# Writing out the expert loop and reordering the first two steps of a Strassen-type mixture-of-experts kernel

## The chip, the cores and the metric

The kernel runs on one core of a Trainium2 chip. The time is the device time of one execution in microseconds (us), lower is better. The comparison is the median of several executions.

## The reference, cut to what matters

The first half of the program is a layer norm and a Fourier-domain cross attention over 32 sequences of 512 rows; the change doesn't touch it. The second half is a mixture of experts. Every token is normalised, sent to the one of 8 experts with the highest logit, if that expert still has room (capacity 1024), run through that expert, scaled by its probability and added to its residual:

```python
h = jax.nn.gelu(jnp.einsum('ech,ehi->eci', dispatch, wi), approximate=False)   # (8,1024,512) x (8,512,2048)
expert_out = jnp.einsum('eci,eih->ech', h, wo)                                  # (8,1024,2048) x (8,2048,512)
combined = weight[:, None] * expert_out[top1, slot]
out = (residual + combined).reshape(inputs.shape)
```

## The kernel before

**Two stages.** The attention stage writes the rows of all tokens, sorted by expert, to `slots` in memory. The function `experts` then opens a block of its own in which each engine has its own instruction stream. All timestamps below from 1973 us on belong to that block.

**Tiling.** An expert's 1024 tokens are two groups of 512 (`n`, `g`), its inner 2048 are eight steps per group (`j`) of two halves of 128. So an expert is 16 steps (`i`), and the stage has 128 steps, numbered `q`. A step's first matrix product (tokens by `wi`) is done as a Strassen-type product of 2 by 2 blocks with seven block products. Each block product is 6 matmuls of 128x128 weights against 256 columns: both operands are split into a high and a low part, and the three products high-high, low-high and high-low run over two slices of the contraction (`product`, L1412). The second product (`down`, L1471 to L1473) is 24 matmuls of 512 columns per step, into the banks `out_ps[0..3]`, which gather over the 8 steps of a group.

**Engines.** TensorE (PE) does the products and turns (transposes) the normalised tokens of the next group (`turn`, L1404), four blocks `c` of four transposes. ScalarE (ACT) rounds operands to their high parts (`weights_high`, `weight_sums_high`, `down_weights_high`, `tokens_high`), normalises (`norm`, L1519), applies gamma and beta to a turned block (`affine`, L1529), copies partial sums between banks (`seed_x`, `seed_w`, `keep_fifth`) and does the gelus. VectorE (DVE) forms the block sums (`weights_add`, L1753 to L1759; `tokens_add`, L1720 to L1725), the low parts (`weights_low` and others) and two additions that close a step (`add_22`, L1788, and `add_12`, L1795). SyncE issues the loads, GpSimd the scattered stores.

**The order within a step** is written out by hand in each engine's `step`. On TensorE step `q` is: `first_products(q)` (12 matmuls, y and v banks), `last_product(q-1)` (6, w bank), `down(q-2)` part 0, a turn in steps 1 to 4 of a group, sixth and second product, `down(q-2)` part 1, the late products, `down(q-2)` parts 2 and 3. `first_products(q)` waits for `add_12(q-1)` and the weights of `q`; `last_product(q)` waits for `add_22(q)`; the turn waits for `fifth_ready(q)`, set by `keep_fifth(q)` behind `seed_x(q)` on ScalarE.

**Loops.** On TensorE, ScalarE, VectorE and SyncE the first and the last expert are written out, and the six between are a loop of the engine (`Fori(1, 7)`) whose body is the 16 steps of one expert. GpSimd has a loop over 7 experts.

**The beginning of the stage.** TensorE marks two banks, then turns the first group's four blocks one after the other through the single bank `v_bank`: block `c+1` waits until ScalarE's `affine` has read block `c`. ScalarE then makes the four high parts of the tokens, VectorE their sums and low parts, and only then do both begin step 0, in which they prepare the weights of step 1.

## Time and profile before

| What | Value |
|---|---|
| Median of 3 executions | 3416.19 us (3410.73 to 3417.0) |
| The profiled execution | 3416.19 us |
| Its span, first to last instruction | 3414.4 us |
| Busy share of TensorE | 96% |
| Mean granted clock of TensorE | 0.984 |

The span is about 1.8 us shorter than the time of the same execution. In the rows below PE is TensorE's matmuls, PEld its weight loads, DVE VectorE, ACT ScalarE, POOL GpSimd. "idle before" is the time in which the engine did nothing before an instruction, with what ended it; "issue" there means that nothing the profile shows was waited for, and PEq is the sequencer of PE. A granted clock of 1.00 is 2.4 GHz and 0.50 is 1.2 GHz.

### The profile page before, as it was taken

The numbers are of one execution on the slowest core, as the hardware profiler recorded it, in microseconds if no ns is written. First come the engines' busy times: TensorE is split into PE (matmuls) and PEld (weight loads), VectorE is DVE, ScalarE is ACT, GpSimd is POOL, SyncE is SP. The second block draws the span as 40 slices with busy tenths as digits, with TensorE's granted clock in tenths as the row PEclk, the third lists the DMA queues.
The fourth block names the chain that finished last, engine by engine and source line by source line (L and its number), as shares of the span: only waits on it lengthen the run. The fifth ranks groups of instructions, "written<-read, shape, count | busy, mean of one in ns | idle before, by whom it ended". The sixth has DMA issues, their size and how long they took to land. (4 is left out here: it accounts for less than half of the span.)

```text
span 3414.4 us, 56375 instructions
## 1 busy us (share of the span) xinstructions
PE 3264.1 (96%) x17944; PEld 2687.3 (79%) x17944; DVE 2868.4 (84%) x3953; ACT 2241.4 (66%) x4838; POOL 1416.3 (41%) x1608
## 2 busy tenths in 40 slices
PE   7999999999999999999999669999999999999998
PEld 5777777777777777777777359998989898989997
DVE  4999999999999999999999757776767776767774
ACT  5666666676666666676666367776767676767764
POOL 3476767677676767676775500000000000000001
PEclk9999999999999999999999779999999999999999
DMA  6422221222121222212120233344434433333331
GB/s 227 148 100 75 88 74 62 74 75 86 62 86 62 87 74 75 92 59 83 62 100 26 75 107 111 109 123 124 125 113 124 125 124 101 112 113 111 123 98 42
DMA packets 299962, 327.61 MB, mean 96 GB/s; under 512 B 47600, under 2 KB 179056, under 8 KB 299760
## 3 DMA queue, kind: packets, MB, share of 16 engines
q1 hardware_dynamic: 284400, 308.12, 28.5%
q0 software_dynamic: 15360, 16.99, 1.4%
q8 instruction: 104, 1.70, 0.2%
q14 instruction: 98, 0.80, 0.1%
HBM read 256.96 MB, written 101.97 MB: 105 GB/s over the span
## 5 line engine op out<-in xcount | busy, mean ns | idle before, releaser
L1369 POOL TENSOR_TENSOR tally<-tally,unit 1x1 f32<-1x1 f32 x16 | 8.4, 523 | 1314.6 <-DVE res L1814 1314.6
L1471 PE MATMUL out_ps<-wo_h,act_h 128*128 128x512 f32 x1024 | 405.1, 396 | 0.0
L1472 PE MATMUL out_ps<-wo_h,act_l 128*128 128x512 f32 x1024 | 404.5, 395 | 0.0
L1473 PE MATMUL out_ps<-wo_l,act_h 128*128 128x512 f32 x1024 | 399.6, 390 | 0.0
L1803 DVE TENSOR_TENSOR act_l<-act,act_h 128x512 fp32r<-128x512 f32 x256 | 176.5, 690 | 257.3 <-ACT act_h L1638 257.2
L1773 DVE TENSOR_TENSOR wi_l<-w_sum,wi_h 128x1024 fp32r<-128x1024 f32 x128 | 156.9, 1226 | 116.5 <-ACT wi_h L1570 115.4
L1412 PE MATMUL y_bank<-tok_h,wi_h 128*128 128x256 f32 x768 | 222.2, 289 | 13.9 <-DVE tok_l L1739 6.3
L972 POOL DMA_INDIRECT slots<-rows,slot_i x128 | 212.3, 1659 | 46.5 <-issue 46.2
L1473 PEld LDWEIGHTS out_ps<-wo_l,act_h 128*128 128x128 f32 x1024 | 193.4, 189 | 43.4
L511 PE MATMUL pair<-w_qh,q_high 128*128 128x512 f32 x512 | 222.2, 434 | 1.5 <-ACT q_low L743 1.5
L1471 PEld LDWEIGHTS out_ps<-wo_h,act_h 128*128 128x128 f32 x1024 | 195.1, 191 | 29.4
L1412 PE MATMUL y_bank<-tok_h,wi_l 128*128 128x256 f32 x768 | 217.5, 283 | 0.0
L1412 PE MATMUL y_bank<-tok_l,wi_h 128*128 128x256 f32 x768 | 217.2, 283 | 0.0
L1472 PEld LDWEIGHTS out_ps<-wo_h,act_l 128*128 128x128 f32 x1024 | 195.0, 190 | 25.9
L737 ACT ACTIVATE c_high<-xt_ps 128x512 fp32r<-128x512 f32 x128 | 76.3, 597 | 207.8 <-PE pair L511 146.3
L511 PE MATMUL pair<-w_vh,c_high 128*128 128x512 f32 x512 | 202.8, 396 | 5.3 <-DVE s L1083 4.1
L511 PE MATMUL pair<-w_kh,c_high 128*128 128x512 f32 x512 | 205.9, 402 | 0.0
L863 POOL TENSOR_TENSOR neg<-sum,minus_inv_dim 128x4 f32<-128x4 f32 x64 | 52.8, 825 | 363.6 <-ACT unused L666 358.0
L511 PE MATMUL pair<-w_ql,q_high 128*128 128x512 f32 x512 | 200.6, 392 | 0.0
L511 PE MATMUL pair<-w_kl,c_high 128*128 128x512 f32 x512 | 200.1, 391 | 0.0
L511 PE MATMUL pair<-w_qh,q_low 128*128 128x512 f32 x512 | 199.8, 390 | 0.0
L511 PE MATMUL pair<-w_vh,c_low 128*128 128x512 f32 x512 | 199.6, 390 | 0.0
(241 smaller groups left out, 11237.1 us busy)
## 6 DMA issues: line engine op xcount, KB each, us to landing
w_raw<-in_L_ffn_wi SPq DMA_DIRECT2D x256, 256.0 KB, 3.0
w_raw<-in_L_ffn_wo SPq DMA_DIRECT2D x128, 512.0 KB, 4.8
w_raw<-in_x SPq DMA_DIRECT2D x32, 1024.0 KB, 5.2
w_raw<-in_ctx SPq DMA_DIRECT2D x32, 1024.0 KB, 5.2
x_res<-in_x SPq DMA_DIRECT2D x31, 1024.0 KB, 5.3
out<-x_res SPq DMA_DIRECT2D x31, 1024.0 KB, 4.4
slots<-rows SPq DMA_DIRECT2D x4, 4160.0 KB, 16.6
got<-slots SPq DMA_DIRECT2D x15, 1040.0 KB, 7.6
```

Source lines behind the costliest of these rows:

```text
L511: last = nc.tensor.matmul(pair[k % 2][:, s, :], spec[:, c, tile * 256 + s * P:tile * 256 + (s + 1) * P], w[:, c, :], start=(c == 0 and n = ...
L737: nc.scalar.activation((c_high, q_high)[w][:, u, :], xt_ps[u % 2][:], ACT.Copy).then_inc(f1_high, 1)
L863: c.step(tv(neg[:], total[:], k["minus_inv_dim"], ALU.mult))
L972: nc.gpsimd.indirect_dma_start(slots, bass.IndirectOffsetOnAxis(ap=slot_i[p][:, t:t + 1].bitcast(u32), axis=0), rows[p][:, t, :], None, bo ...
L1369: nc.gpsimd.tensor_tensor(tally[:], tally[:], unit[:], ALU.add).then_inc(tallied, 1)
L1412: last = nc.tensor.matmul(dst, x[w][:, a, k, :], y[g][:, b, k, :], start=start and k == 0 and x is wi_h and y is tok_h, stop=False, skip_g ...
L1471: nc.tensor.matmul(out_ps[t][:], ah, oh, start=(j == 0 and h == 0), stop=False)
L1472: nc.tensor.matmul(out_ps[t][:], al, oh, start=False, stop=False)
L1473: last = nc.tensor.matmul(out_ps[t][:], ah, ol, start=False, stop=(j == STEPS - 1 and h == 1))
L1773: v.tensor_tensor(wi_l[i % 2][:, 3:7], w_sum[:], wi_h[i % 2][:, 3:7].bitcast(f32), ALU.subtract).then_inc(wi_low, 1)
L1803: v.tensor_tensor(act_l[i % INNER_RING][:, two], act32[:, two], act_h[i % INNER_RING][:, two].bitcast(f32), ALU.subtract).then_inc(done, 1)
```

## The change

It has four parts.

1. TensorE, ScalarE and VectorE get all 8 experts written out (`for e in range(EXPERTS)` of the program text in place of the engine's loop). SyncE and GpSimd keep their loops.
2. The first group's four turned blocks go to four banks, `out_ps[0..3]`, which nothing else uses yet, so a block no longer waits for the one before to be read. ScalarE applies gamma and beta to blocks 0 and 1, VectorE to blocks 2 and 3 (`affine_first`). `tokens_high` part 0 of group 0 now waits for all four blocks, and `tokens_add(0)` stands ahead of `tokens_low(0, 0, 0)`.
3. The work for step 1's weights moves from step 0 to before it: `weights_add(1)` ahead of `affine_first` on VectorE, `weights_high(1)` between the tokens' high parts on ScalarE, `weights_low(1)` behind the tokens' low parts.
4. For steps 0 and 1 (`CLOSED = 2`) TensorE runs `last_product(q)` at the end of step `q`'s late products, and not after the first products of step `q+1`.

```diff
--- before.py
+++ after.py
@@ -1308,6 +1308,7 @@
         res_ready, mixed_ready, mixed_stored = sem("res_ready"), sem("mixed_ready"), sem("mixed_stored")
 
         LAST = EXPERTS * 2 * STEPS
+        CLOSED = 2
 
         def on(q):
 
@@ -1395,13 +1396,14 @@
                     first = isinstance(n, int) and n == 0
                     if not first:
                         pe.wait_ge(normed_ready, n * GT + GT)
-                    wait(pe, tok_ready, n * CB + c)
                     if not first:
+                        wait(pe, tok_ready, n * CB + c)
                         pe.wait_ge(fifth_ready, q + 1)
+                    bank = out_ps[c] if first else v_bank
                     for t in range(GT):
                         if first and c == 0:
                             pe.wait_ge(normed_ready, t + 1)
-                        last = nc.tensor.transpose(v_bank[:, t * P:(t + 1) * P], normed[:, t, c * P:(c + 1) * P], eye[:])
+                        last = nc.tensor.transpose(bank[:, t * P:(t + 1) * P], normed[:, t, c * P:(c + 1) * P], eye[:])
                     last.then_inc(tr_mm, 1)
 
                 def product(dst, q, i, a, b, start=False):
@@ -1479,7 +1481,8 @@
                     before, early = (i - 1) % 16, (i - 2) % 16
                     n_early = e * 2 + (i - 2) // STEPS
                     first_products(q, n, i)
-                    last_product(q - 1, before)
+                    if q - 1 >= CLOSED:
+                        last_product(q - 1, before)
                     down(q - 2, n_early, early, 0)
                     if on(q) and 1 <= j <= CB:
                         turn(n + 1, j - 1, q)
@@ -1487,19 +1490,17 @@
                     second_product(q, i)
                     down(q - 2, n_early, early, 1)
                     late_products(q, i)
+                    if q < CLOSED:
+                        last_product(q, i)
                     down(q - 2, n_early, early, 2)
                     down(q - 2, n_early, early, 3)
 
                 mark_banks()
                 for c in range(CB):
                     turn(0, c, 0)
-                for i in range(16):
-                    step(0, i)
-                with pe.Fori(1, EXPERTS - 1) as e:
+                for e in range(EXPERTS):
                     for i in range(16):
                         step(e, i)
-                for i in range(16):
-                    step(EXPERTS - 1, i)
                 step(EXPERTS, 0)
                 step(EXPERTS, 1)
 
@@ -1526,14 +1527,15 @@
                     act.wait_ge(tr_mm, n * CB + c + 1)
                     if c == 0:
                         wait(act, tok_low, n * 4 - 1)
-                    nc.scalar.activation(tok32[:, c, :], v_bank[:], ACT.Identity, bias=bet[:, c:c + 1],
+                    bank = out_ps[c] if isinstance(n, int) and n == 0 else v_bank
+                    nc.scalar.activation(tok32[:, c, :], bank[:], ACT.Identity, bias=bet[:, c:c + 1],
                                          scale=gam[:, c:c + 1]).then_inc(tok_ready, 1)
 
                 def tokens_high(n, g, part):
                     if not group_on(n):
                         return
                     if part == 0:
-                        act.wait_ge(tok_ready, n * CB + 2)
+                        act.wait_ge(tok_ready, n * CB + (4 if isinstance(n, int) and n == 0 else 2))
                         wait(act, p4_mm, (n - 1) * STEPS)
                         nc.scalar.activation(tok_h[g][:, B21:B22 + 1], halves(tok32[:, 0:2, :]), ACT.Copy).then_inc(tok_high, 1)
                     elif part == 1:
@@ -1656,7 +1658,8 @@
                     inner_high(q - 1, before, 0)
                     gelu_21(q - 1)
                     inner_high(q - 1, before, 1)
-                    weights_high(q + 1, after)
+                    if q > 0:
+                        weights_high(q + 1, after)
                     seed_w(q, i)
                     gelu_11(q)
                     weight_sums_high(q + 1, after)
@@ -1686,19 +1689,14 @@
                 norm(0, 0)
                 affine(0, 0)
                 affine(0, 1)
-                affine(0, 2)
-                affine(0, 3)
                 tokens_high(0, 0, 0)
                 tokens_high(0, 0, 1)
+                weights_high(1, 1)
                 tokens_high(0, 0, 2)
                 tokens_high(0, 0, 3)
-                for i in range(16):
-                    step(0, i)
-                with act.Fori(1, EXPERTS - 1) as e:
+                for e in range(EXPERTS):
                     for i in range(16):
                         step(e, i)
-                for i in range(16):
-                    step(EXPERTS - 1, i)
                 step(EXPERTS, 0)
 
             @block.vector
@@ -1708,6 +1706,11 @@
                 def halves(rows):
 
                     return bass.AP(rows.tensor, rows.offset, [list(rows.ap[0]), [TOK, 2], [GROUP, 2], [1, TOK]])
+
+                def affine_first(c):
+                    dve.wait_ge(tr_mm, c + 1)
+                    v.tensor_scalar(tok32[:, c, :], out_ps[c][:], gam[:, c:c + 1], bet[:, c:c + 1],
+                                    ALU.mult, ALU.add).then_inc(tok_ready, 1)
 
                 def tokens_add(n):
 
@@ -1818,8 +1821,9 @@
                     q = e * 16 + i
                     j, g, n = i % STEPS, i // STEPS, e * 2 + i // STEPS
                     before, after = (i - 1) % 16, (i + 1) % 16
-                    weights_add(q + 1, after, 0)
-                    weights_add(q + 1, after, 1)
+                    if q > 0:
+                        weights_add(q + 1, after, 0)
+                        weights_add(q + 1, after, 1)
                     inner_low(q - 1, before, 0)
                     if j == 2:
                         mix(n - 1, 1 - g, (2, 3))
@@ -1836,7 +1840,8 @@
                     inner_low(q - 1, before, 1)
                     if j == 1:
                         mix(n - 1, 1 - g, (0,))
-                    weights_low(q + 1, after)
+                    if q > 0:
+                        weights_low(q + 1, after)
                     weight_sums_low(q + 1, after)
                     add_22(q, i)
                     add_12(q, i)
@@ -1849,18 +1854,19 @@
                 weights_low(0, 0)
                 weight_sums_low(0, 0)
                 down_weights_low(0, 0)
+                weights_add(1, 1, 0)
+                weights_add(1, 1, 1)
+                affine_first(2)
+                affine_first(3)
+                tokens_add(0)
                 tokens_low(0, 0, 0)
-                tokens_add(0)
                 tokens_low(0, 0, 1)
                 tokens_low(0, 0, 2)
                 tokens_low(0, 0, 3)
-                for i in range(16):
-                    step(0, i)
-                with dve.Fori(1, EXPERTS - 1) as e:
+                weights_low(1, 1)
+                for e in range(EXPERTS):
                     for i in range(16):
                         step(e, i)
-                for i in range(16):
-                    step(EXPERTS - 1, i)
                 for i in range(3):
                     step(EXPERTS, i)
```

## Rows read from the trace of the kernel before

**Rows 1.** The page, busy time and instructions, and the granted clock in 40 slices.

```profile
PE 3264.1 (96%) x17944; PEld 2687.3 (79%) x17944; DVE 2868.4 (84%) x3953; ACT 2241.4 (66%) x4838; POOL 1416.3 (41%) x1608
...
PEclk9999999999999999999999779999999999999999
```

**Rows 2.** Waits, engine PE, 2020 to 3414 us: total, times, longest.

```profile
PE v_bank L1412 <- issue: 12.1, 5, 2.9
PE y_bank L1412 <- issue: 3.1, 5, 0.9
```

**Rows 3.** Stretches; columns: length, busy (instructions) by engine, PEclk, DMA share, GB/s.

```profile
2013.00:2016.00 3.00, 3.00 (x12) 2.71 (x12) 1.40 (x4) 2.15 (x5) 0.00 (x0) 0.50 0.84 230
2150.00:2325.00 175.00, 175.00 (x1105) 158.05 (x1104) 127.79 (x207) 125.60 (x228) 12.98 (x10) 1.00 0.38 115
2337.00:2343.00 6.00, 3.34 (x20) 3.15 (x19) 1.98 (x5) 1.46 (x4) 0.00 (x0) 0.78 0.56 147
3220.00:3376.00 156.00, 156.00 (x988) 141.22 (x986) 109.07 (x174) 108.11 (x198) 12.69 (x10) 1.00 0.32 94
```

**Rows 4.** Timeline, PE: start us, us, instruction, [idle before it <- releaser].

```profile
2046.67 0.28 PE L1412 MATMUL v_bank<-tok_h,wi_h 128*128 128x256 f32 x1
...
2164.35 0.28 PE L1412 MATMUL v_bank<-tok_h,wi_h 128*128 128x256 f32 x1
...
2218.78 0.28 PE L1412 MATMUL v_bank<-tok_h,wi_h 128*128 128x256 f32 x1
...
2336.80 0.38 PE L1412 MATMUL y_bank<-tok_h,wi_h 128*128 128x256 f32 x1 [0.90 <-issue]
...
2340.91 0.37 PE L1412 MATMUL v_bank<-tok_h,wi_l 128*128 128x256 f32 x1 [2.66 <-issue]
...
3219.75 0.28 PE L1412 MATMUL v_bank<-tok_h,wi_h 128*128 128x256 f32 x1
```

**Rows 5.** DMA queues, 2165 to 2335 us, the two of instruction code: packets, MB, share.

```profile
q8 instruction: 9, 0.15, 0.4%
q14 instruction: 9, 0.07, 0.1%
```

**Rows 6.** Waits, engine DVE, 2020 to 3380 us.

```profile
DVE w_sum L1753 <- issue: 27.2, 5, 6.4
```

**Rows 7.** Timeline, PE, the start of the expert stage.

```profile
1979.79 0.48 PE L1404 MATMUL v_bank<-eye,normed 128*128 128x128 f32 x1 [0.23 <-ACT normed L1519]
...
1985.10 1.12 PE L1404 MATMUL v_bank<-eye,normed 128*128 128x128 f32 x4 [0.87 <-ACT tok L1529]
1992.52 0.55 PE L1412 MATMUL y_bank<-tok_h,wi_h 128*128 128x256 f32 x1 [6.30 <-DVE tok_l L1739]
...
2001.56 0.35 PE L1412 MATMUL y_bank<-tok_h,wi_h 128*128 128x256 f32 x1 [2.96 <-DVE pre L1795]
...
2011.09 0.36 PE L1412 MATMUL y_bank<-tok_h,wi_h 128*128 128x256 f32 x1 [1.56 <-DVE pre L1795]
```

**Rows 8.** Timeline, ACT, the start of the expert stage.

```profile
1991.80 1.06 ACT L1545 ACTIVATE tok_h<-normed 128x1024 fp32r<-128x1024 f32 x1 [0.27 <-DVE normed L1725]
...
1995.74 0.84 ACT L1563 ACTIVATE wi_h<-w_raw 128x768 fp32r<-128x768 f32 x1
...
2001.77 2.92 ACT L1519 ACTIVATE normed<-got 128x512 f32<-128x512 f32 x4
2004.59 0.36 ACT L1584 ACTIVATE x_bank<-y_bank 128x256 f32<-128x256 f32 x1
```

**Rows 9.** Timeline, DVE, the start of the expert stage.

```profile
1988.01 1.22 DVE L1739 TENSOR_TENSOR tok_l<-tok,tok_h 128x1024 fp32r<-128x1024 f32 x1 [9.65 <-ACT tok_h L1538]
1989.15 0.68 DVE L1720 TENSOR_TENSOR normed<-tok 128x512 f32<-128x512 f32 x1
...
2000.67 0.41 DVE L1788 TENSOR_TENSOR pre<-fifth,w_bank 128x256 f32<-128x256 f32 x1
```

**Rows 10.** Groups by form, DVE, whole span: busy us, mean ns, idle before.

```profile
L1166 DVE TENSOR_TENSOR rows<-rows,odd_ps 128x512 f32<-128x512 f32 x64 | 44.0, 688 | 5.3 <-PE odd_ps L545 2.0
```

## The prediction

> **What bounds the kernel now.** I read the page first. TensorE is busy for 96% of the span, and the granted clock is full nearly everywhere, so TensorE's own stream sets the time and only its idle stretches and its slow-clock stretches can be won [rows 1]. The page has one dent, where the attention stage ends and the expert stage begins. The next view is TensorE's waits from 2020 us on, that is for the expert stage without its start. In nearly 1400 us the list has just two entries: five waits before a matmul into the v bank, 12.1 us together, and five before one into the y bank, 3.1 us together, all of them "issue", which means that no other engine was waited for [rows 2]. Five is the number of times that a loop over six experts jumps back. The stretches say the same from the other side: from 2150 to 2325 us and from 3220 to 3376 us TensorE is busy for every microsecond at full clock, and from 2337 to 2343 us it is busy for 3.34 of 6 us at a clock of 0.78 [rows 3]. The timeline there shows both waits of one jump: 0.90 us before the first product of the expert, and 2.66 us in the middle of a product, between two matmuls of the same accumulation, where no semaphore stands [rows 4]. So the engine lacked instructions.
>
> **What is done by the change, part by part.**
>
> *1. The loop.* What a jump costs is more than its idle time, as the clock falls behind it, so I take it from the pitch of the experts. The first v-bank matmul of step 5 stands at 2046.67 us and that of step 21 at 2218.78 us. The 16 steps between them lie in the written-out expert and in the loop's first pass, across its entry, and took 172.11 us. Six experts at that pitch are 1032.66 us. The looped ones, from step 16 at 2164.35 us to step 112 at 3219.75 us, took 1055.40 us [rows 4]. The difference, 22.7 us, is what five jumps cost: 15.2 us of idle time [rows 2] and 7.5 us of matmuls at half clock and of work that ran late. VectorE sits idle for 27.2 us at the same five places [rows 6]. It counts nothing of its own, as the pitch includes what it did to TensorE. Is all of it won? Each engine runs as many work instructions as before, so what the jumps' place is taken by is code that is read in order. Such code is there to be looked at: in 2150 to 2325 us TensorE idles for nothing, while 18 packets of instruction code arrive in 170 us of it [rows 3, 5], and in the last expert (3220 to 3376 us) it idles for nothing either [rows 3]. The bounds are 15.2 us (the clock is lost to something else) and 22.7 us. I take 22.7, as the written-out stretches run at full clock throughout.
>
> The loops that stay cost nothing today: SyncE's and GpSimd's jump as before, and at TensorE's waits no DMA is named [rows 2]. Within the stage there is no shorter chain behind TensorE that would take over, for the 172.11 us are its own matmuls.
>
> *Against a rule.* [Rows 4] show 3.56 us of idle time at one jump. The Trainium skill, "Advanced Engine Details and Errata", section "Control Flow Timing", gives about 51 ns for an unconditional branch and 108 ns for one with a comparison. By that, an estimate from the page alone, five jumps would be some 0.5 us, and the sum of this part 0.5 in place of 22.7. The trace disagrees about what happens at these places; whether it is the jump that does it, the change decides (rival 3).
>
> *2. Turning the first group in four banks.* Now block c waits for ScalarE's read of block c-1: 0.87 us idle before the last block of four transposes, which starts at 1985.10 us and takes 1.12 us [rows 7]. That is (1.12 - 0.48) / 3 = 0.213 us per transpose plus a tail of 0.48. Block 0 stays where it is, for it waits for the normalised tokens one by one (its last transpose starts at 1979.79 us). Twelve more transposes without a wait end at 1979.79 + 12 x 0.213 + 0.48 = 1982.83 us, where before it was 1986.22. The trace has no `affine` on VectorE. The nearest row is a two-operand operation of 128x512 with a PSUM source, 0.688 us [rows 10]. It could be a little shorter, and a doubling would cost 0.7 us. I take 0.69, so both of VectorE's blocks are done at 1982.83 + 0.05 + 0.69 = 1983.6 us, and ScalarE's two are done before that. The four operations of `weights_add(1)` moved ahead of it on VectorE run while ScalarE normalises and TensorE transposes block 0, a time in which VectorE has nothing else. They cost nothing unless they last beyond the arrival of block 2, and each is half the size of the 0.68 us operations of `tokens_add` [rows 9].
>
> *3. The tokens.* `tokens_add(0)` starts at 1983.65 in place of 1989.15 us. From its start to TensorE's first product it was 1992.52 - 1989.15 = 3.37 us. Now the first low part, which stood ahead of it, stands behind it, and its pitch of 1989.15 - 1988.01 = 1.14 us is added [rows 7, 9]. The first product is then due at 1983.65 + 3.37 + 1.14 = 1988.16 us, which is 4.4 us earlier. ScalarE's high parts (at most 1.06 us each) with `weights_high(1)` between them (0.84 us [rows 8]) start at the same moment as `tokens_add` and are each shorter than VectorE's low parts (up to 1.22 us [rows 9]), so VectorE, which has the sums to make first, stays behind them and they are hidden. What would be queued behind `tokens_high` part 0, with its new wait for all four blocks, is `weights_high(1)`, and nobody wants that before step 1.
>
> *4. Step 0.* It loses `weights_add(1)`, `weights_high(1)` and `weights_low(1)`. The chain that ended it was on ScalarE and VectorE: copy of y into the w bank, loading of the gelu table, gelu, high part of the sums, their low part, the two closing additions at 2000.67 us, and TensorE's next product at 2001.56 us after 2.96 us of idle time [rows 7, 8, 9]. `weights_high(1)` stood directly ahead of that chain, so between 0 and 0.84 us of it is won. I take 0.1, near nothing, as the copy itself waits for TensorE's sixth product.
>
> *5. Closing steps 0 and 1 at once.* The six matmuls need `add_22` alone, and TensorE idled until `add_12` came: 2.96 us before step 1 and 1.56 us before step 2 [rows 7]. They start one addition earlier, by 2001.56 - (2000.67 + 0.41) - 0.1 = 0.4 us. In step 1 this wins nothing: ScalarE normalises group 1 (2.92 us) and only then, at 2004.59 us, makes the copy that the turn waits for [rows 8]. Even at half clock (0.213 us each, 18 matmuls, 3.8 us) the products are done about when that copy is. In step 2 TensorE has no more gaps behind its start, so 0.4 us counts there.
>
> *6. The clock at the start.* From 2013 to 2016 us TensorE is fully busy at 0.50, which costs 1.5 us [rows 3]. It follows the idle stretches of steps 0 and 1, and the change shortens these. It can win up to 1.5 us, or lose as much if the slow stretch falls on the products that the first two steps now hold. I take 0.
>
> The sum is 22.7 + 4.4 + 0.1 + 0.4 = 27.6 us. The profiled execution took 3416.19 us, the same as the median, so the forecast is 3416.2 - 27.6 = **3388.6 us**. Attention and the tail (stores behind the last product) are not touched.
>
> **The rivals.**
>
> *Rival 1: the start gives nothing*, since its chain is kept by another wait, for example a DMA, or ScalarE's high parts. Then 3416.2 - 22.7 = 3393.5 us. Against it speaks that the 6.30 us of idle time before the first product are put down to VectorE's low part [rows 7].
>
> *Rival 2: only the short wait is the jump's*, and the longer one in mid-product is a place where the code runs out anyway. For it speaks that it comes after some ten matmuls of the body, and not at its head. Against it speaks the loop's first pass, which has the same body and no such wait (the pitch of 172.11 us covers it [rows 4]). 22.7 x 3.1 / 15.2 = 4.6 us are won there, with 4.9 at the start: 3406.7 us.
>
> *Rival 3: the loop is worth only the branches*, and the code runs out at each expert's beginning, written out or not. Then only the start counts: 3411.3 us, by the skill's figures 3410.8. The entries into the second and last expert, both passed at full pitch [rows 3, 4], speak against it.
>
> *Rival 4, slower: code read in order stalls too.* The mechanism is that each packet of code that arrives keeps TensorE waiting. At the rate of [rows 5] the stage has 18 / 170 x 1353 = 143 packets. Priced like the mean short wait, 3.1 / 5 = 0.62 us [rows 2], that is 89 us more, so 3477 us. It decides from (27.6 + 6.8) / 143 = 0.24 us per packet on. Against it: 18 packets in a stretch without idle time.
>
> *Rival 5: the slow-clock stretch at the start goes too*: 3387.1 us.
>
> **How the numbers follow.** The forecast gets 0.76, rival 5 0.09, rival 1 0.06, rival 2 0.04, rival 3 0.02 and rival 4 0.03. The forecast and rival 5 cover 3383 to 3393 with their unknowns (1.5 us of clock either way, 0.7 us of `affine_first`, 1 us each for the chain of step 0 and for the jumps, and the runs of before spread by 6.3 us). Taking in rival 1 and some of this spread, the range is 3380 to 3398 us. A measurement of this kernel tells about 0.2% (6.8 us) from no change, so faster means under 3409.4 us: all but rivals 3 and 4, with a little off for surprises, 0.94. Rival 3 makes 0.03 for the same, and rival 4 0.03 for slower.
>
> **What the profile after would show.** If part 1 is right, TensorE's waits from 2020 us on have no "issue" entry left, VectorE's 27.2 us are gone, and eight experts follow each other at 172.1 us. If parts 2 and 3 are right, the first product stands near 1988.2 us and the turned blocks end near 1982.8 us. If parts 4 and 5 are right, the product of step 1 that ends the long idle time is one into the w bank, near 1996.6 us, and the first of step 2 (now at 2011.09) is one near 2006.1 us, so that from step 3 on everything stands 4.9 us earlier. The prediction is wrong if TensorE waits for "issue" at new places, if the clock stays at 0.50 over most of the first two steps, or if VectorE's `affine_first` is far longer than 0.69 us.

## The result

The changed kernel takes 3389.28 us (median of 4 executions, 3387.07 to 3390.92), the kernel before beside it 3415.68 us (median of 4, one more than in the table above). The ratio is 0.9925, with a 95% interval of 0.9908 to 0.9942, so it is faster by 0.6 to 0.9%. The forecast was 3388.6 us.

The page of the kernel after (span, busy time, granted clock in 40 slices):

```profile
span 3385.0 us, 55016 instructions
...
PE 3253.7 (96%) x17944; PEld 2682.1 (79%) x17944; DVE 2870.0 (85%) x3955; ACT 2238.7 (66%) x4836; POOL 1415.9 (42%) x1608
...
PEclk9999999999999999999999879999999999999999
```

The span is 29.4 us shorter than before, more than the medians differ (26.4 us). Part of that is chance: the expert stage began 0.76 us earlier, though nothing ahead of it was changed, and over the thirteen profiles of this study with an unchanged attention stage (all but the one of the long attention body) its first instruction stood anywhere between 1972.16 and 1976.62 us. So everything below is counted from the stage's own beginning, TensorE's first matmul in it, at 1973.32 us before and 1972.56 us after. The texts call it the stage's first instruction.

TensorE's waits after, from 2015 to 3414 us. This is the whole answer, the head of the list and nothing under it, where [rows 2] had two entries:

```profile
core 0 of [0], span 3385.0 us
engine line waited for: us in total, times, longest us
```

The stretches after (length, busy time and instructions by engine, granted clock, DMA share, GB/s):

```profile
2002.00:2005.00 3.00, 3.00 (x15) 3.00 (x15) 1.93 (x3) 2.61 (x5) 0.00 (x0) 0.50 0.18 66
2006.00:2018.00 12.00, 11.73 (x76) 10.68 (x77) 9.91 (x18) 8.30 (x16) 0.00 (x0) 1.00 0.34 96
2329.00:2335.00 6.00, 6.00 (x43) 5.53 (x42) 2.88 (x5) 4.03 (x9) 0.00 (x0) 1.00 0.67 180
```

The kernel before had a slow stretch (granted clock 0.50) in step 1 too, beside the one of [rows 3] in step 2:

```profile
2003.00:2005.00 2.00, 2.00 (x10) 1.74 (x9) 0.98 (x3) 2.00 (x5) 0.00 (x0) 0.50 0.59 176
```

Counted from the stage's beginning its slow stretches lie at 29.1 to 32.5 us and at 39.3 to 42.8 us. After, there is one, at 29.1 to 32.5 us. The one in step 2 is gone.

The last row of the stretches after holds the beginning of the third expert, the place that [rows 3] show at 2337 us with 3.34 of 6 us busy and a clock of 0.78. Now it is full.

The timeline of TensorE after, the first v-bank matmuls of step 16 and of step 112:

```profile
2157.69 0.28 PE L1414 MATMUL v_bank<-tok_h,wi_h 128*128 128x256 f32 x1
...
3190.33 0.28 PE L1414 MATMUL v_bank<-tok_h,wi_h 128*128 128x256 f32 x1
```

3190.33 - 2157.69 = 1032.64 us for six experts, where [rows 4] had 1055.40. The prediction's undisturbed pitch gave 1032.66.

The start of the stage after, TensorE, then VectorE, then ScalarE (start, duration, instruction, idle time before it and what ended it):

```profile
1979.03 3.03 PE L1406 MATMUL out_ps<-eye,normed 128*128 128x128 f32 x13 [0.23 <-ACT normed L1520]
1987.45 0.55 PE L1414 MATMUL y_bank<-tok_h,wi_h 128*128 128x256 f32 x1 [5.39 <-DVE tok_l L1742]
...
1996.28 0.39 PE L1414 MATMUL w_bank<-tok_h,wi_h 128*128 128x256 f32 x1 [2.54 <-DVE pre L1791]
...
2000.54 0.63 PE L1406 MATMUL v_bank<-eye,normed 128*128 128x128 f32 x4 [1.85 <-ACT fifth L1593]
...
2006.27 0.38 PE L1414 MATMUL w_bank<-tok_h,wi_h 128*128 128x256 f32 x1 [0.69 <-DVE pre L1791]
```

```profile
1981.25 1.67 DVE L1712 TENSOR_SCALAR tok<-out_ps,gam,bet 128x512 f32<-128x512 f32 x2 [2.18 <-PE out_ps L1406]
1982.95 0.69 DVE L1723 TENSOR_TENSOR normed<-tok 128x512 f32<-128x512 f32 x1
...
1995.81 0.41 DVE L1791 TENSOR_TENSOR pre<-fifth,w_bank 128x256 f32<-128x256 f32 x1
```

```profile
1996.91 2.92 ACT L1520 ACTIVATE normed<-got 128x512 f32<-128x512 f32 x4
1999.73 0.36 ACT L1586 ACTIVATE x_bank<-y_bank 128x256 f32<-128x256 f32 x1
```

Compare with [rows 7]. The reader sees in the first line 13 transposes in one go, the last one of block 0 and the twelve of the other blocks, which had been held apart by ScalarE. The first product comes 1987.45 - 1972.56 = 14.89 us after the stage's first instruction, where it was 1992.52 - 1973.32 = 19.20 us. The idle time before step 1 is ended by `add_22` (VectorE, L1791), and the instruction that it releases is a product into the w bank, the one that closes step 0.

### The profile page after: what moved, and what is told of

Read it like the earlier page. It is cut to its first block and busy times, and to the rows that moved or that the text cites. A ratio compares the mean times of both kernels' runs of the same rounds, so it can differ in the third digit from the quotient of the medians.

```text
span 3385.0 us, 55016 instructions
## 1 busy us (share of the span) xinstructions
PE 3253.7 (96%) x17944; PEld 2682.1 (79%) x17944; DVE 2870.0 (85%) x3955; ACT 2238.7 (66%) x4836; POOL 1415.9 (42%) x1608
## 5 line engine op out<-in xcount | busy, mean ns | idle before, releaser
L1473 PEld LDWEIGHTS out_ps<-wo_h,act_h 128*128 128x128 f32 x1024 | 193.7, 189 | 29.1
```

The source lines that it names most:

```text
L1473: nc.tensor.matmul(out_ps[t][:], ah, oh, start=(j == 0 and h == 0), stop=False)
```

## The experiments

Three numbers are compared for each kernel: the time, the stretch from step 16 to step 112 (the six experts), and the start, which is from the stage's first instruction to the first v-bank matmul of step 16 (191.0 us before, 185.1 us after).

**The loops alone.** All three loops of the kernel before are written out:

```diff
-                for i in range(16):
-                    step(0, i)
-                with pe.Fori(1, EXPERTS - 1) as e:
-                    for i in range(16):
-                        step(e, i)
-                for i in range(16):
-                    step(EXPERTS - 1, i)
+                for e in range(EXPERTS):
+                    for i in range(16):
+                        step(e, i)
```

(and the same on ScalarE and VectorE)

> The kernel before with the three loops over experts written out and nothing else. Theory (the jumps cost 22.7 us and are gone): the time falls by 22.7 us, to about 3393 us, TensorE has no issue wait from 2020 us on, and steps 16 to 112 take 1032.7 us instead of 1055.4. Rival (part of the gain came from the new start, for example through the clock): less than 20 us.

The median is 3393.81 us against 3413.77 (ratio 0.994, 0.9924 to 0.9957), the six experts take 1032.64 us, and no issue wait is left. The stage's own measure is as forecast to 0.1 us. The median gain of 20.0 us is 2.7 us short of it, within what the interval allows (15 to 26 us), and it sits on the rival's border of 20 us. The rival's cause isn't seen, though: the six experts alone gain 22.8 us between the profiles, without the new start.

**The start alone.** The changed kernel with the three loops put back, and the conditions on `q` made for the written-out steps only:

```diff
-                for e in range(EXPERTS):
-                    for i in range(16):
-                        step(e, i)
+                for i in range(16):
+                    step(0, i)
+                with pe.Fori(1, EXPERTS - 1) as e:
+                    for i in range(16):
+                        step(e, i)
+                for i in range(16):
+                    step(EXPERTS - 1, i)
...
-                    if q < CLOSED:
+                    if isinstance(q, int) and q < CLOSED:
```

> The changed kernel with the loops put back, so only the start is new. Theory (the parts add up): 5 to 6 us faster than before, about 3410 us, with step 3 some 5.9 us earlier after the stage's first instruction, and the five pairs of issue waits still there, 20 to 25 us in steps 16 to 112. Rival (the start's gain needs the written-out code): under 3 us.

It took 3410.2 us against 3413.77 (ratio 0.9989, 0.998 to 0.9999, that is 0.3 to 7 us). The expectation was 5 to 6 us, so the median came out short, though the interval covers it. The start takes 185.0 us, as in the changed kernel, 6.1 us less than in the kernel before. The jumps' waits are back, in the profile of this kernel (TensorE, 2020 to 3380 us; total, times, longest):

```profile
PE v_bank L1414 <- issue: 10.1, 5, 2.3
PE y_bank L1414 <- issue: 2.6, 5, 0.7
```

Its six experts take 1052.0 us, so five jumps cost 19.3 us here, a little below the forecast 20 to 25. The two halves of the change do add up, 20.0 + 3.6 = 23.6 us by the medians against 26.4 for both, with the difference well inside the intervals.

**TensorE's loop alone, and the other two alone.** As in the first experiment, but on TensorE only:

> The kernel before with TensorE's loop written out, ScalarE's and VectorE's kept. Theory A (TensorE's own lack of code is the whole cost): steps 16 to 112 take 1032.7 us, as with all three written out. Theory B (VectorE's jump, 5.3 us idle each time, is a cost of its own that TensorE's wait hides): TensorE now waits for VectorE's additions at the five places, 1 to 3 us each, so 1038 to 1050 us.

The median is 3394.02 us (ratio 0.9942, 0.9925 to 0.9958) and the six experts take 1032.63 us. So theory A holds, and the 1 to 3 us of theory B don't appear. VectorE's waits of this kernel, 2020 to 3380 us:

```profile
DVE w_sum L1749 <- issue: 24.3, 5, 5.1
```

and its timeline at the first of the five places:

```profile
2337.58 0.43 DVE L1749 TENSOR_TENSOR w_sum<-w_raw 128x256 f32<-128x256 f32 x1 [4.99 <-issue]
...
2339.06 1.28 DVE L1799 TENSOR_TENSOR act_l<-act,act_h 128x512 fp32r<-128x512 f32 x2
```

VectorE still sits idle for 4.2 to 5.1 us at each jump. It then finds its inputs ready (the two low parts behind follow without the usual wait for ScalarE). Its closing additions come 1.1 us late in this step (2342.34 us, 11.63 us behind those of the step before, where the kernel with all three loops written out takes 10.54 us) and are level again in the next, and TensorE never waits for them. VectorE is busy for only some 70 to 75% of a stretch [rows 3]. The mirror image, ScalarE and VectorE written out and TensorE's loop kept:

> The kernel before with ScalarE's and VectorE's loops written out, TensorE's kept. Theory A (TensorE's own lack of code is the whole cost): steps 16 to 112 stay at 1055 us and TensorE keeps its 15 us of issue waits. Rival (VectorE's late start is the larger part): 1045 us or less.

3413.73 us against 3413.77 (ratio 1.0, 0.9991 to 1.001): nothing, with the six experts at 1051.8 us. That is 3.6 us less than in the kernel before. The next experiment shows how much the price of a jump varies. The waits of TensorE in this kernel:

```profile
PE v_bank L1412 <- issue: 10.7, 5, 2.4
PE y_bank L1412 <- issue: 1.7, 5, 0.6
```

So the whole gain of the loops is TensorE's, and writing out the other two is worth nothing that the timing can show.

**Two experts per pass.** In the kernel before, on all three engines:

```diff
-                with pe.Fori(1, EXPERTS - 1) as e:
+                with pe.Fori(1, EXPERTS - 1, 2) as e:
                     for i in range(16):
                         step(e, i)
+                    for i in range(16):
+                        step(e + 1, i)
```

> The kernel before with two experts written out per pass of the loop: three passes, two jumps back. Theory (each jump costs the same): steps 16 to 112 take 1032.7 + 2 x 4.55 = 1041.8 us and the time falls by 13.6 us, to 3402 us. Rival (the cost is of the body's length, not of the jumps): no change.

3402.99 us against 3414.63 (ratio 0.9964, 0.9951 to 0.9977), six experts in 1042.9 us (1041.8 expected). The median falls by 11.6 us, 2 us less than the theory's 13.6. TensorE's waits in this kernel:

```profile
PE v_bank L1412 <- issue: 4.5, 2, 2.4
PE y_bank L1412 <- issue: 1.0, 2, 0.7
```

Two of each in place of five. The cost goes with the jumps. A jump costs 5.1 us here, 4.6 in the kernel before, and 3.9 and 3.8 in the two kernels above that kept TensorE's loop. Over the 17 jumps of these four profiles it is 4.2 us, and a single one is 2.4 to 6.0 us.

Much of that difference is the clock. In the kernel before, around the first and the third jump:

```profile
2338.00:2345.00 7.00, 4.34 (x22) 3.87 (x21) 3.22 (x7) 2.83 (x6) 0.00 (x0) 0.76 0.29 76
2691.00:2698.00 7.00, 5.17 (x36) 4.83 (x37) 3.00 (x7) 3.28 (x7) 0.00 (x0) 1.00 0.59 157
```

At the first the granted clock falls to 0.50 for 3.4 us, and the pass takes 5.2 us longer than the undisturbed 172.11. At the third it stays full, and the pass takes 2.5 us longer. All 17 jumps fall into these two kinds: twelve with a slow stretch of 3.4 us (once 6.8) cost 4.1 to 6.0 us, 4.8 in the mean, and five without one 2.4 to 3.3 us, 2.8 in the mean.

**Is every jump this dear?** TensorE's loop in the attention stage jumps back too, and shows no issue wait. The changed kernel, its DMA queues from 600 to 1700 us (packets, MB, share), in which the two queues of instruction code don't occur at all:

```profile
q1 hardware_dynamic: 49198, 78.26, 21.3%
q0 software_dynamic: 5831, 4.29, 1.2%
```

The experiment makes that body twice as long, in the changed kernel:

```diff
-                    with pe.Fori(6, 30, 2) as b:
-                        body(b, 0)
-                        body(b + 1, 1)
+                    with pe.Fori(6, 30, 4) as b:
+                        for k in range(4):
+                            body(b + k, k % 2)
```

> The changed kernel with TensorE's loop of the attention stage holding four sequences per pass in place of two. Between 600 and 1700 us that loop jumps every two sequences, shows no issue wait, and no packet of code arrives at all. Theory (a jump is free as long as the body is still in the engine's own store, and costs a fetch when it is too long for it): code packets arrive in the attention stage and TensorE shows issue waits of 1 to 4 us at the five jumps, in part hidden behind VectorE. Rival (the attention stage's jumps are free for another reason): nothing changes there.

In the same 1100 us, which hold four of the five jumps, 54 packets of code now arrive. Over the whole attention stage the five jumps show:

```profile
q8 instruction: 54, 0.88, 0.3%
```

```profile
PE xt_ps L488 <- issue: 13.2, 5, 3.0
```

2.6 us each, like the longer wait of [rows 2]. The theory holds: the short body was still there when TensorE jumped back to it, and the long one had to be fetched again. Counted in the traces, a pass of the short body is some 1220 instructions of TensorE (576 matmuls, as many weight loads and the sequencer's own), one of the long body 2428, and a pass of the loop over the experts in the kernel before 2269. So the body that stalls there is about as long as the one made to stall here. In time it is hardly seen. The median is 3389.33 us against 3414.63, a ratio of 0.9924, and the changed kernel's was 3389.28. The stalls took the place of waits that were there anyway: from 600 to 1700 us TensorE's waits for VectorE's rows (L545) are 12.6 us in the changed kernel and 3.4 us in this one, and VectorE is busy for 1084 of these 1100 us in the changed kernel.

In the kernel before, the code that arrived over the expert stage (2027 to 3380 us) was

```profile
q8 instruction: 78, 1.28, 0.4%
q14 instruction: 71, 0.58, 0.1%
```

and in the kernel after

```profile
q8 instruction: 67, 1.10, 0.3%
q14 instruction: 39, 0.32, 0.1%
```

With TensorE's loop alone written out the first queue shows 67 packets and the second 71, with ScalarE's and VectorE's alone 79 and 39. So q8 carries TensorE's code and q14 that of ScalarE and VectorE, and each jump makes TensorE fetch two to four packets that code read in order doesn't need (11 and 12 more for five jumps, 7 more for the two jumps of two experts per pass).

**The parts of the start.** Three kernels each undo one part in the changed kernel. Each has one execution, so they are compared by stretches of their profiles and not by the time. `CLOSED = 0`:

> The changed kernel with CLOSED = 0, so the last product of steps 0 and 1 stands where it did. Theory of the prediction: 0.4 us worse at step 3, nothing before. Theory of the clock: the six matmuls moved into the idle stretches also keep the slow-clock stretch out of step 2; without them TensorE falls to half clock in step 2 again and step 3 comes 1.5 to 2.3 us later.

The start takes 185.4 us, where it took 185.1. Step 3 comes 45.81 us after the stage's first instruction against 45.51 us. The second theory of this expectation is wrong: TensorE kept its full clock in step 2 here (the wait before step 2 is 1.57 us, as before, and step 2 takes 11.07 us), so the closing of the steps is not what keeps the slow stretch out of step 2. The clock was full in step 1 as well, from 19.0 us into the stage on, where the changed kernel's profile has its slow stretch. So the two profiles differ in more than the closing. In both profiles of the changed kernel the product that ends the idle time before step 1 comes 8.83 to 8.88 us behind the first one, and here 9.29 us, which is the 0.4 us of the prediction. At step 3 the difference is 0.3 us against the first of these profiles and 0.9 us against the second (the run again, below, with a full clock in steps 1 and 2).

One bank (`bank = v_bank` on TensorE and ScalarE, TensorE's wait for the block before, `affine(0, 2)` and `affine(0, 3)` on ScalarE in place of `affine_first`, `tokens_high` part 0 waiting for two blocks):

> The changed kernel with the first group's turned blocks in one bank and all four read by ScalarE, as before. Theory: TensorE's first product comes later after the stage's first instruction by about 3.4 us (19.2 us before, 14.9 us after, and 1.1 us of the difference is not from the banks but has the other sign). Rival (the order of the sums and low parts made the gain): under 1.5 us later.

The first product comes at 18.78 us in place of 14.89. In this kernel's timeline of TensorE the last block and the first product are

```profile
1988.93 1.12 PE L1406 MATMUL v_bank<-eye,normed 128*128 128x128 f32 x4 [0.87 <-ACT tok L1531]
1995.40 0.55 PE L1414 MATMUL y_bank<-tok_h,wi_h 128*128 128x256 f32 x1 [5.35 <-DVE tok_l L1744]
```

with the 0.87 us in front of the block that [rows 7] show. The start is 4.5 us longer. Not all of the 3.9 us between 18.78 and 14.89 is the banks'. In this profile ScalarE waited for the landing of the third part of the group's rows:

```profile
1981.86 1.71 ACT L1520 ACTIVATE normed<-got 128x512 f32<-128x512 f32 x2 [0.24 <-DMA got<-slots]
```

Block 0's last transpose starts 7.00 us into the stage here and 6.47 us in the kernels before and after, so 0.5 us is that landing's and the four banks are worth 3.4 us, the theory's figure. The rest of the 4.3 us that the first product gained lies behind the turned blocks: from the end of the last one to the first product TensorE waits 6.30 us in the kernel before, 5.39 us after and 5.35 us here, where the blocks are in one bank but the sums still stand ahead of the first low part. So the new order of the sums is worth 0.9 us.

The weights of step 1 back in step 0:

```diff
-                    if q > 0:
-                        weights_high(q + 1, after)
+                    weights_high(q + 1, after)
...
-                weights_add(1, 1, 0)
-                weights_add(1, 1, 1)
```

(and likewise `weights_low` and VectorE's `weights_add` in the step)

> The changed kernel with all of step 1's weight work back in step 0. Theory of the prediction: moving it won about 0.1 us, so step 1 starts 0.1 us later against the first product. Rival (ScalarE's copy into the w bank was held by it, or the first product is held by it where it stands now): a difference of over 0.5 us either way.

The first product stands at 14.90 us, step 16 at 185.12 us, both within 0.01 us of the changed kernel, in one profile of each. This part is worth nothing. The copy into the w bank began at 1991.69 us, 4.16 us behind the first product, and in the changed kernel 4.17 us behind it.

**Going further.** In the changed kernel ScalarE's four normalising instructions of group 1 stand between step 0 and the copy that step 1's turn waits for. Three of them can stand in step 0:

```diff
                     seed_x(q, i)
+                    if spread:
+                        norm(1, 1, (0,))
                     keep_fifth(q, i)
+                    if spread:
+                        norm(1, 1, (1,))
...
+                    if spread:
+                        norm(1, 1, (2,))
                     gelu_22(q)
```

> The changed kernel with three of the four normalising instructions of group 1 moved into ScalarE's idle places in step 0, since in step 1 TensorE waits 1.85 us for the copy that stands behind them. Theory: the turn of step 1 starts 1.6 us earlier and the whole stage with it, about 0.05% of the time, more than a profile needs but less than the timing resolves. Rival: the copies between them come late and step 0 gets as much longer.

3386.24 us against 3415.26 (ratio 0.9917, 0.9901 to 0.9934). The turn of step 1 starts 27.35 us into the stage, where the changed kernel had 27.98: 0.6 us and not 1.6. TensorE's wait for ScalarE before the turn is down from 1.85 to 0.56 us. ScalarE now waits itself, for products that fell into a stretch of slow clock (a row of ScalarE's timeline, then a stretch):

```profile
1999.94 0.38 ACT L1593 ACTIVATE fifth<-v_bank 128x256 f32<-128x256 f32 x1 [0.91 <-PE v_bank L1414]
```

```profile
1998.00:1999.00 1.00, 1.00 (x6) 1.00 (x6) 1.00 (x3) 0.37 (x2) 0.00 (x0) 0.50 0.00 0
```

The start takes 184.2 us, 1.0 us less than the mean of 185.2 us over four profiles of the changed kernel's start order (itself, the start alone, the long attention body, and the changed kernel once more, below). Those four lie between 184.6 and 186.2 us, so one profile alone doesn't show the 1.0 us. From the first product to step 16 the difference stands out better: 169.3 us here and in the last kernel below, 169.8 to 170.8 us in the four.

Last, the changed kernel was run again beside one that also lets each of the last four stores wait for its own addition:

```diff
-                    pool.wait_ge(mixed_ready, n * GT + GT)
+                    last = isinstance(n, int) and n == EXPERTS * 2 - 1
+                    pool.wait_ge(mixed_ready, n * GT + (1 if last else GT))
...
                     for t in range(GT):
+                        if last and t:
+                            pool.wait_ge(mixed_ready, n * GT + t + 1)
```

(GpSimd's loop ends one expert earlier for it)

> The changed kernel once more, as the partner of the next run on the same chip. Theory (the gain of the start is 4.9 us, and the 5.9 us of the profile shown has chance in it, from where TensorE's clock falls): steps 16 to 112 take 1032.6 us again, and step 16 comes 185 to 186.2 us after the stage's first instruction.

> The changed kernel with the normalising spread over step 0 as in the run before, and in the last group of the last expert each of the four stores waits for its own addition and not for all four. Theory: 1.0 us at the start; at the end the stores are 1.28 us apart and the additions 1.36 us, so three of the stores move ahead of the last addition and 3.8 us are won. Together 4.8 us faster than the changed kernel, about 3384.5 us. Rival (the last store's own landing sets the end and starts no earlier, or GpSimd waits elsewhere): 1 us.

The changed kernel took 3387.25 us (0.9923 of before, 0.991 to 0.9937), its six experts 1032.63 us and its start 184.6 us, a little below the stated 185 to 186.2. The further one took 3381.95 us (0.9914, 0.99 to 0.9927), 5.3 us less on the same chip, though the two intervals overlap. By the profiles the 5.5 us between the two spans are 3.85 us at the end, 0.3 us at the start (184.3 against 184.6 us, not the 1.0 us of the theory) and 1.35 us from an expert stage that began earlier, with the same attention stage ahead of it. So the sum of 4.8 us was met with 1.35 us of chance in it. GpSimd's first and last store of the last group, in the run of the changed kernel and in the further one:

```profile
3373.76 0.99 POOL L1372 DMA_INDIRECT out<-res,meta  x1 [0.54 <-issue]
...
3377.61 0.97 POOL L1372 DMA_INDIRECT out<-res,meta  x1 [0.30 <-issue]
```

```profile
3368.11 0.99 POOL L1375 DMA_INDIRECT out<-res,meta  x1 [0.55 <-issue]
...
3372.11 0.97 POOL L1375 DMA_INDIRECT out<-res,meta  x1 [0.39 <-issue]
```

From the first v-bank matmul of step 127 to the end of the span it was 34.8 us, and now it is 31.0: 3.8 us, as forecast. This kernel has the lowest median of the study.

## Why the prediction was right

**1. The loop** was forecast at 22.7 us and measured in the profile at 22.8 (1055.40 against 1032.64 us). The step that carried it was to take the price from the pitch of the experts and not from the 15.2 us of idle time. The loops alone gave 20.0 us by the medians. That is part of the same finding: the profiled execution of before was somewhat dear (4.6 us per jump, where the mean over 17 jumps is 4.2, so about 21 us for five). In that profile the clock fell behind four of the five jumps, in the two other kernels with five jumps behind three. The 7.5 us that the prediction put down to half clock and late work fits: four slow stretches of 3.4 us at half clock, with half of each lost, are 6.8 us.

**2. The four banks.** The turned blocks were due 1982.83 - 1973.32 = 9.51 us into the stage and were done at 1979.03 + 3.03 - 1972.56 = 9.50 us. `affine_first` takes 0.81 us and not 0.69, a term off by 0.1 us, and the sums behind it began 0.06 us later than forecast (10.39 against 10.33 us into the stage).

**3. The tokens.** The first product was due 14.84 us into the stage and came at 14.89. Of the 4.3 us the banks are 3.4 (12.90 - 9.50 us for the end of the turned blocks), and the order of the sums is 0.9, by the trace of the kernel with one bank.

**4. The moved weights** were priced at 0.1 us of a possible 0.84, and are worth nothing. The copy waited for TensorE's sixth product, as the prediction said.

**5. Closing the steps** was priced at 0.4 us. The kernel without it starts step 1 by 0.4 us later and is 0.3 or 0.9 us later at step 3, according to which profile of the changed kernel it is held against. The reason why step 1 itself wins nothing holds too: from `add_22` of step 0 to the turn it is 4.73 us before and after, all on ScalarE's path. (The copy that the turn waits for is the one into `fifth`, right behind the row that the prediction names, which is the copy into the x bank.)

**6. The clock** was put at 0, between a gain and a loss of 1.5 us. Here luck has a part. The forecast's two marks in between were missed by a little: into the stage, the product that ends the idle time before step 1 was due at 23.3 us and came at 23.72, and the one before step 2 was due at 32.8 and came at 33.71. At the second mark the changed kernel was 4.1 us ahead and not 5.0. The clock took part in that: behind the first product it rose to full after 4.0 us, where it had taken 3.1 us before, and the slow stretch of step 1 now fell behind the turn, where products follow without a wait, and no longer in front of it, where TensorE has to wait for the copy anyway. Step 2 then passed at full clock and gave 1.8 us back, and from step 3 on the profile is 5.9 us ahead, which lies between the forecast (4.9) and rival 5 (6.4).

The change's order can't be given the credit for the missing slow stretch: of the five profiles with the start of the kernel before, three have none in step 2 either (that step took 11.07 us from v bank to v bank, where the kernel before took 12.6). Those three took 189.7, 190.1 and 190.0 us for the start, the other two, the loops alone and the kernel before itself, 191.1 and 191.0. On the other side, none of the nine profiles with the new start, whole or in part, has one in step 2. Whether that is chance stays open. The five average 190.4 us, the four with the new start 185.2, and the difference is 5.2 us, where the sum without the clock said 4.9. Against the three without the slow stretch it is 4.7 us.

**The total.** 27.6 us were forecast and 26.4 measured, with an interval of 20 to 31 us. That the time itself came within 0.7 us of the forecast is closer than the runs can tell: the loops' term rests on a profile with somewhat dear jumps, the start gave a little more than its terms, and the kernel before was 0.5 us faster in its four executions than in the profiled one. What the runs do bear out is the two terms that make the sum, each by itself.

**Rivals.** Rival 1 (the start gives nothing) falls by the start alone and by the profile. Rival 2 (only the short wait is the jump's) and rival 3 (the code runs out in any case) fall by the empty list of waits. The runs also show that the Trainium skill's price of a branch, some 0.1 us ("Advanced Engine Details and Errata", "Control Flow Timing"), isn't what an expert's jump costs: the attention stage's short loop jumps at no visible cost, and what costs 4.2 us is the code that must come again. The trace agrees with the Trainium skill's "Runtime: NRT & Kernel Launch", section "Instruction fetch mechanics": the fetch runs ahead in order, and a taken branch to code that is no longer held waits for it. How much is held that section gives in two ways, as a window of two pages of 256 instructions and as 2048 instructions for TensorE. The trace fits the second: some 1220 instructions came back without a fetch, 2269 and 2428 didn't. The 67 packets of code read in order cost no wait, and the 17 jumps cost 2.4 to 6.0 us each. Rival 4 (code read in order stalls) falls too: 67 packets of TensorE's code arrive in 1353 us, and TensorE waits for none.

## What to carry to other kernels

A loop of an engine is free while its body is still held by the engine at the jump back, and costs some microseconds per pass once it is too long. Two signs tell the cases apart in a profile before anything is changed: packets of instruction code in the stage of the loop (alone they prove nothing, as code read in order brings them too, 67 in this stage), and waits put down to "issue" at the same place of each pass. Only the engine that sets the pace pays (here TensorE; VectorE's stall of 4.2 to 5.1 us was swallowed by its slack), and the price is read from the pitch of undisturbed passes, as it holds the clock that falls behind the stall and not only the idle time.

When the first and last pass are written out anyway, their pitch shows what the written-out middle will do, as it did here (172.11 us in both).

## What the runs showed of the hardware

- TensorE's body of two sequences in the attention stage is passed without a packet of code in 1100 us, and one of four sequences brings 54 packets and waits of 2.6 us a jump. In instructions of TensorE these are some 1220 and 2428, and the expert's body, which stalls, has 2269. The edge lies between 1220 and 2269; where, these runs don't tell.
- The same jump is not equally dear each time: 2.4 to 3.3 us where the granted clock stayed at 1.00 (5 jumps), 4.1 to 6.0 us where it fell to 0.50 for 3.4 us, once for 6.8 (12 jumps). The runs without jumps also lie closer together: 3410.73 to 3417.0 us before, 3387.07 to 3390.92 after.
- VectorE's affine operation with two per-partition scalars on 128x512 from PSUM took 0.81 us, and the additions of that size with a PSUM source take 0.69 us [rows 10].
- Behind the first product of the stage TensorE has idle stretches of 1 to 3 us in the first steps. In 10 of the 14 profiles its granted clock falls to 0.50 there once or twice, for 3.4 or 6.8 us. In the other four (TensorE's loop alone written out, ScalarE's and VectorE's alone, `CLOSED = 0`, the changed kernel once more) it stays full once it has risen, in spite of idle stretches of 2.3 to 2.9 us. The same code at the start does either, and what decides was not settled.
